# Attention and a soft mixture of experts on one core: where the next batch's rows are turned, which engine rotates the first head, and where one row maximum stands

## The chip, the cores and the metric

The kernel runs on one core of a Trainium2 chip. The metric is device time in microseconds, from the start of the program to its end. Times of single instructions come from one profiled execution.

## What is computed

Two blocks, each followed by a residual sum and a layer norm, on x of 8 batches, 1024 tokens, 128 features. The first is causal attention of 8 heads of width 128 with rotary embedding, the second a soft mixture of experts with 512 slots and a hidden width of 512. Cut to what matters:

```python
q, k, v = (einsum('bim,mhd->bhid', x, w) for w in (wq, wk, wv))
q, k = rope(q), rope(k)          # halves swapped, times sin, plus times cos
s = einsum('bhid,bhjd->bhij', q, k) / 128
p = softmax(s - 1e30 * (i < j))
x = layernorm(x + einsum('bhij,bhjd,hdm->bim', p, v, wo))
xn, se = rms_norm(x, gamma_x), rms_norm(slot_embeds, gamma_slot)
logits = einsum('bsd,etd->bset', xn, se)
slots = einsum('bsd,bset->betd', xn, softmax(logits, axis=1))
out = einsum('bnd,bsn->bsd', gelu(slots @ w1) @ w2, softmax(logits.reshape(b, s, 512)))
x = layernorm(x + out)
```

## The kernel before, in words

`attention_block` goes through 64 heads (8 batches of 8) in a pipeline, written out step by step and not as a loop on the chip. Each engine has a function `step(head)` that lists its own instructions for that step in order; the engines meet only through semaphores. So the order within each `step` is the schedule. `before` and `after` are the heads one step earlier and later. The work of a head is spread over two steps.

Products that need float32 accuracy are made of a high and a low part: ScalarE copies a PSUM result into the high part (`..._hi`), VectorE subtracts that from the same PSUM bank to get the low part (`..._lo`), and TensorE does three matmuls (`matmul_split`, L53 to L57). A PSUM bank is free for TensorE once VectorE has made the low part.

For one head, TensorE makes k and q (`project_k`, `project_q`), and their rotation is done outside: SyncE's queue swaps the halves by DMA (`swap`, L336), GpSimd multiplies k by the cosine, both swapped parts by the sine, adds, and makes both low parts (`mul_sin` L424, `rotate_add` L432, `split_lo` L440, each on 128x1024 elements). The scores of the eight row tiles of 128 queries come in fills: "s4", "s7", "s6", "s5", "s10" (tiles 1 and 0) and, in the next step, "s32". VectorE takes the row maximum (`rowmax`, L629) and ScalarE the exponential (`exp`, L511). TensorE turns the probabilities block by block (`turn`, L845) into the two banks of `ps_turn`; the fills are named "5b", "4a", "7a", "2", "5a", "3", "10", "4b", "7b", "6b", "6a" in their order, and banks alternate. Their high and low parts (L556, L656) go to `weigh_high`, `weigh_split` and `weigh_low`, which multiply by V.

V is made together with the output weights: their product is `wvo`, and `project_v` makes V for two heads. It needs x transposed, `kept.x_t`, in two copies, one for this batch and one for the next. The next batch's rows are loaded by SyncE in a batch's first step (L376). In the step of its third head (`loads_x`, `X_STEP` 2), the eight blocks are turned by `turn_x` (L853) in two halves of four blocks, into the same two banks of `ps_turn`: the first half at the end of that step, the second in the next step ahead of the scores "s32". ScalarE and VectorE split them (`split_x_hi` L561, `split_x_lo` L682), and turns "5b" and "4a" of that head come behind them, each behind a wait for `x_lo` (L919 to L922). This happens for batches 0 to 6, seven times.

Ahead of the first step stand the loading and splitting of weights, the turning of the first x, the making of `wvo`, and the first head's k, q and rotation. GpSimd does that rotation in the same order as later ones (L493 to L501).

`ffn_block` goes through 8 batches. In each, VectorE takes 8 row maxima (`find_row_peak`, L1354), the one of tile t after ScalarE's exponentials of that tile (`disped`), and between them scales the next batch's rows in two halves (`scale_rows`, L1332), behind a wait for GpSimd's norm (`norm1_known`). TensorE turns tile t once maximum t-2 is there (`turn_tile`, L1479), and turns the scaled rows of the next batch (`z_transposes`, L1465) after `z_made`, the first half after maximum 6, the second after maximum 7.

## Time and profile before

| | |
|---|---|
| median of 3 runs | 1693.78 us (1693.4 to 1696.32) |
| the profiled execution | 1695.32 us |
| its span | 1693.5 us |
| instructions | 30814 |
| TensorE busy | 1641.3 us |
| GpSimd busy | 1416.9 us |
| VectorE busy | 1217.5 us |
| ScalarE busy | 1216.6 us |
| DMA | 133.96 MB, mean 79 GB/s |

The span runs from the first to the last instruction of the profiled execution. PE is TensorE's matmuls, PEld its weight loads (they overlap), DVE VectorE, ACT ScalarE, POOL GpSimd, SP SyncE. A line of the timeline gives the start in the span, the duration, engine, line of the kernel, operation, output and inputs with shapes, the number of like instructions merged, and in brackets how long the engine was idle before and what released it. Matmuls are pipelined: one that shows 0.40 us begins 0.23 us after the one before it.

### The profile page before, as it was taken

To read this page: it belongs to the slowest core of one execution; us is meant where nothing else is said; L and a number is where in the kernel's file an instruction comes from. 1 tells how busy PE (TensorE), PEld (TensorE's weight loads), DVE (VectorE), ACT (ScalarE), POOL (GpSimd) and SP (SyncE) were. 2 spreads that over 40 slices of the span, in tenths; PEclk is the share of its full clock that TensorE was granted. 3 is DMA by queue.
4 is the path that set the end of the run, shared out by engine and by line. 5 is a ranking of instruction groups with operands and counts; after the bars stand their busy time and mean duration, and the time that the engine had idled before them with its cause. 6 is when DMAs were issued, how large, how long until landed. Compare 5 with 4: busy or idle time off the path is not lost. (4 is left out here: it accounts for less than half of the span.)

```text
span 1693.5 us, 30814 instructions
## 1 busy us (share of the span) xinstructions
PE 1641.3 (97%) x10524; PEld 1478.0 (87%) x10524; DVE 1217.5 (72%) x2891; ACT 1216.6 (72%) x2425; POOL 1416.9 (84%) x802
## 2 busy tenths in 40 slices
PE   5999999999999999999999999999999998999997
PEld 4888888888888888888888888888888886899997
DVE  3777776777777777776777777777777777677875
ACT  3777777777777777777777777777777764665664
POOL 5889988998899889998999899989988974777784
PEclk9999999999999999999999999999999999999999
DMA  4222232223222322232223222322232323223212
GB/s 146 78 70 74 76 101 62 73 78 101 62 76 75 101 73 75 75 100 76 75 75 100 75 76 76 100 76 75 75 88 76 88 76 94 51 62 94 68 31 57
DMA packets 76489, 133.96 MB, mean 79 GB/s; under 512 B 19264, under 2 KB 45888, under 8 KB 76352
## 3 DMA queue, kind: packets, MB, share of 16 engines
q1 hardware_dynamic: 74880, 130.10, 28.6%
q10 hardware_dynamic: 1472, 2.10, 0.4%
q8 instruction: 78, 1.28, 0.3%
q14 instruction: 59, 0.48, 0.1%
HBM read 56.36 MB, written 8.70 MB: 38 GB/s over the span
## 5 line engine op out<-in xcount | busy, mean ns | idle before, releaser
L511 ACT ACTIVATE probs<-ps_slot,neg_max 128x640 f32<-128x640 f32 (+7 forms) x512 | 379.3, 742 | 139.1 <-DVE neg_max L629 139.1
L629 DVE CUSTOM_DVE_ANT_0 ps_slot<-ps_slot,causal 128x640 f32<-128x640 f32 (+7 forms) x512 | 385.8, 763 | 73.3 <-PE ps_slot L57 73.3
L845 PE MATMUL ps_turn<-ident,probs 128*128 128x128 f32 x2304 | 320.4, 274 | 12.6 <-DVE x_t L682 7.6
L845 PEld LDWEIGHTS ps_turn<-ident,probs 128*128 128x128 f32 x2304 | 264.2, 140 | 43.7 <-DVE x_t L682 9.3
L55 PE MATMUL ps_slot<-k,q 128*128 128x512 f32 (+4 forms) x768 | 280.9, 366 | 2.8 <-issue 2.0
L57 PE MATMUL ps_slot<-k,q 128*128 128x512 f32 (+4 forms) x768 | 263.8, 344 | 0.0
L56 PE MATMUL ps_slot<-k,q 128*128 128x512 f32 (+4 forms) x768 | 262.8, 342 | 0.0
L656 DVE TENSOR_TENSOR pt_split<-ps_turn,pt_split 128x512 fp32r<-128x512 f32 x256 | 175.3, 685 | 93.4 <-ACT pt_split L556 93.4
L440 POOL TENSOR_TENSOR q<-rot_q,q 128x1024 fp32r<-128x1024 f32 x64 | 153.8, 2403 | 64.4 <-ACT q L539 64.4
L656 DVE TENSOR_TENSOR pt_high<-ps_turn,pt_high 128x128 fp32r<-128x128 f32 (+3 forms) x256 | 124.3, 486 | 114.5 <-ACT pt_high L556 114.5
L424 POOL TENSOR_TENSOR swapped_k<-swapped_k,rope 128x1024 f32<-128x1024 f32 x64 | 153.8, 2402 | 55.4 <-DMA swapped_k<-unrot_k 55.4
L418 POOL TENSOR_TENSOR rot_k<-unrot_k,rope 128x1024 f32<-128x1024 f32 x64 | 154.0, 2406 | 17.2 <-ACT unrot_k L521 16.6
L432 POOL TENSOR_TENSOR rot_q<-rot_q,swapped_q 128x1024 f32<-128x1024 f32 x64 | 152.7, 2386 | 9.9 <-POOL swapped_q L424 1.0
L432 POOL TENSOR_TENSOR rot_k<-rot_k,swapped_k 128x1024 f32<-128x1024 f32 x64 | 153.1, 2392 | 9.2
L55 PEld LDWEIGHTS ps_slot<-k,q 128*128 128x128 f32 x768 | 145.7, 190 | 15.5 <-issue 3.7
L556 ACT ACTIVATE pt_high<-ps_turn 128x128 fp32r<-128x128 f32 (+3 forms) x256 | 112.3, 439 | 63.9 <-PE ps_turn L845 57.8
L57 PEld LDWEIGHTS ps_slot<-k,q 128*128 128x128 f32 x768 | 144.9, 189 | 14.6
L56 PEld LDWEIGHTS ps_slot<-k,q 128*128 128x128 f32 x768 | 145.7, 190 | 11.8
L556 ACT ACTIVATE pt_split<-ps_turn 128x512 fp32r<-128x512 f32 x256 | 147.6, 602 | 10.5 <-PE ps_turn L845 10.4
L440 POOL TENSOR_TENSOR k<-rot_k,k 128x1024 fp32r<-128x1024 f32 x64 | 154.3, 2411 | 0.0
L424 POOL TENSOR_TENSOR swapped_q<-swapped_q,rope 128x1024 f32<-128x1024 f32 x64 | 153.5, 2399 | 0.0
L456 POOL TENSOR_TENSOR y_sum<-y_sum,y_head 128x1024 f32<-128x1024 f32 x55 | 131.8, 2396 | 19.3 <-issue 19.3
(174 smaller groups left out, 4300.0 us busy)
## 6 DMA issues: line engine op xcount, KB each, us to landing
swapped_k<-unrot_k SPq DMA_DIRECT2D x128, 256.0 KB, 3.6
swapped_q<-unrot_q SPq DMA_DIRECT2D x128, 256.0 KB, 3.7
inv_b<-inv_rows SPq DMA_DIRECT2D x64, 512.0 KB, 4.7
x_rows<-in_L_attn_x SPq DMA_DIRECT2D x8, 512.0 KB, 5.8
y_t<-y_sum SPq DMA_DIRECT2D x8, 512.0 KB, 5.4
x_rows<-y_t SPq DMA_DIRECT2D x8, 512.0 KB, 3.5
unrot_q<-in_L_attn_x SPq DMA_DIRECT2D x8, 512.0 KB, 5.0
row_b<-r_rows SPq DMA_DIRECT2D x16, 256.0 KB, 3.4
```

Of the source, the lines that this page charges most:

```text
L55: pe.matmul(out, stat_hi, mov_hi, start=start, stop=False, skip_group_check=True)
L56: pe.matmul(out, stat_hi, mov_lo, start=False, stop=False, skip_group_check=True)
L57: return pe.matmul(out, stat_lo, mov_hi, start=False, stop=stop, skip_group_check=True)
L418: pool.tensor_tensor(rot[1][:, :], unrot[1][:, :], kept.rope[:, 0, :], ALU.mult).then_inc(cos_made[1], 1)
L424: pool.tensor_tensor(swapped[which][:, :], swapped[which][:, :], kept.rope[:, 1, :], ALU.mult).then_inc(sin_made[which], 1)
L432: pool.tensor_tensor(rot[which][:, :], rot[which][:, :], swapped[which][:, :], ALU.add).then_inc(rotated[which], 1)
L440: pool.tensor_tensor(out[:, 1, :], rot[which][:, :], f32(out[:, 0, :]), ALU.subtract)\
L511: act.activation(probs_tile(t), score_tile(name, head, i), ACT.Exp, scale=-1.0, bias=neg_max[:, head.par, t:t + 1], accum_out=sums[:, head ...
L556: last = act.activation(hi, src, ACT.Copy)
L629: dve.tensor_tensor_reduce(tile, tile, causal[:, T - WIDTH[t]:T], -1.0, UNSEEN, ALU.add, ALU.min, neg_max[:, head.par, t:t + 1]).then_inc( ...
L656: last = dve.tensor_tensor(lo, src, f32(hi), ALU.subtract)
L845: last = pe.transpose(bank[:, at:at + P], probs_tile(t)[:, j * P:(j + 1) * P], ident[:, :])
```

## The change

In the attention half `turn_x` does both halves in one place, behind the scores "s6" of the third head's own step, in the banks that "3" and "10" of the head before have left; TensorE then waits for both low parts ahead of turn "4b". ScalarE and VectorE split the halves behind the exponentials of tile 7 and the row maximum of tile 6. The special cases in the next step, and the late "5b", are gone. In the first head, the products by the sine, the additions and the low parts of k and q go from GpSimd to VectorE, with the splits of the first V in between; ScalarE makes k's high part ahead of V's, and starts the loads of wv and wo only when the first x has landed. In the feed-forward half, row maximum 5 stands ahead of the first half of the scaling and 6 ahead of the second.

```diff
--- before.py
+++ after.py
@@ -320,7 +320,7 @@
         both_turn = ps_turn[:, :, :].rearrange("p g c -> p (g c)")
 
         def x_bank(head, half):
-            return ps_turn[:, (head.at + 1 + half) % 2, :]
+            return turn_bank(("3", "10")[half], head.step(-1))
 
         def x_half(head, half, part):
             return kept.x_t[(head.at // 8 + 1) % 2][:, part, half * BANK:(half + 1) * BANK]
@@ -493,12 +493,6 @@
             first = Head(0, 0, heads)
             pool.wait_ge(rope_landed, 32)
             mul_cos_k(first)
-            mul_sin(1, first)
-            rotate_add(1, first)
-            mul_sin(0, first)
-            rotate_add(0, first)
-            split_lo(1, first)
-            split_lo(0, first)
             steps(pool, step, 16)
 
         @block.scalar
@@ -560,8 +554,10 @@
                 act.wait_ge(x_turned, head.batch() * 2 + (half + 1))
                 act.activation(x_half(head, half, 0), x_bank(head, half), ACT.Copy).then_inc(x_hi, 1)
 
-            for n, w in (("k", wk), ("q", wq), ("v", wv)):
+            for n, w in (("k", wk), ("q", wq)):
                 act.dma_start(w_raw[n], w.rearrange("m h d -> m (h d)")).then_inc(w_landed[n], 16)
+            act.wait_ge(first_x_landed, 16)
+            act.dma_start(w_raw["v"], wv.rearrange("m h d -> m (h d)")).then_inc(w_landed["v"], 16)
             act.dma_start(w_raw["o"].rearrange("p (h m) -> p h m", h=H), wo.rearrange("h d m -> d h m"))\
                .then_inc(w_landed["o"], 16)
             act.wait_ge(first_x_turned, 1)
@@ -573,19 +569,15 @@
             act.activation(wv_t, both_turn, ACT.Copy).then_inc(wv_copied, 1)
             act.wait_ge(wvo_made, 1)
             act.activation(wvo_part(0), both_y, ACT.Copy).then_inc(wvo_hi, 1)
+            split_hi(1, first)
             split_v_hi(first.step(-2))
             split_v_hi(first.step(-1))
-            split_hi(1, first)
 
             def step(head):
                 before, after = head.step(-1), head.step(1)
                 if before.live():
                     split_v_hi(before)
-                if loads_x(before):
-                    split_x_hi(before, 1)
                 split_hi(0, head)
-                if loads_x(before):
-                    turn("5b", before)
                 turn("4a", before)
                 turn("7a", before)
                 exp("s32", before, 1)
@@ -601,6 +593,9 @@
                     act.wait_ge(z_turned, 1)
                     act.activation(kept.z_t[:, 0, :], z_slot, ACT.Copy).then_inc(z_hi, 1)
                 exp("s7", head)
+                if loads_x(head):
+                    for half in range(2):
+                        split_x_hi(head, half)
                 exp("s6", head)
                 turn("4b", head, high_done)
                 turn("7b", head)
@@ -610,10 +605,7 @@
                 exp("s10", head, 1)
                 exp("s10", head, 0)
                 turn("6a", head, split_done)
-                if loads_x(head):
-                    split_x_hi(head, 0)
-                else:
-                    turn("5b", head)
+                turn("5b", head)
 
             steps(act, step, 16)
 
@@ -716,6 +708,9 @@
                 if is_step(head, heads):
                     split_slots()
                 rowmax("s6", head)
+                if loads_x(head):
+                    for half in range(2):
+                        split_x_lo(head, half)
                 if is_step(head, heads - 1):
                     dve.wait_ge(tokens_added, 1)
                     for t in range(NT):
@@ -737,10 +732,7 @@
                         dve.tensor_tensor_reduce(kept.se_sq[:, c, :], kept.se_raw[:, c, :], kept.se_raw[:, c, :], 1.0, 0.0,
                                                  ALU.mult, ALU.add, kept.stats[:, 1, c, 0:1]).then_inc(se_squared, 1)
                 turn("6a", head)
-                if loads_x(head):
-                    split_x_lo(head, 0)
-                else:
-                    turn("5b", head)
+                turn("5b", head)
                 scale_y(1, before)
                 if is_step(head, heads):
                     dve.wait_ge(z_hi, 1)
@@ -749,14 +741,8 @@
                     dve.wait_ge(w1_hi, 1)
                     dve.tensor_tensor(kept.w1_s[:, 1, :], kept.w1_raw, f32(kept.w1_s[:, 0, :]), ALU.subtract)\
                        .then_inc(w1_lo, 1)
-                if loads_x(head):
-                    split_v_lo(head)
-                    split_x_lo(head, 1)
-                    rowmax("s32", head, 1)
-                    turn("5b", head)
-                else:
-                    split_v_lo(head)
-                    rowmax("s32", head, 1)
+                split_v_lo(head)
+                rowmax("s32", head, 1)
                 rowmax("s32", head, 0)
                 turn("4a", head)
                 scale_y(0, before)
@@ -770,6 +756,21 @@
                 dve.scalar_tensor_tensor(kept.w[:, :, lo, :], raw_w, scale, f32(kept.w[:, :, hi, :]),
                                          ALU.mult, ALU.subtract).then_inc(w_lo[n], 1)
 
+            def first_rotation(which):
+                dve.wait_ge(swap_landed[which], 32)
+                dve.tensor_tensor(swapped[which][:, :], swapped[which][:, :], kept.rope[:, 1, :],
+                                  ALU.mult).then_inc(sin_made[which], 1)
+                dve.wait_ge(sin_made[which], 1)
+                dve.wait_ge(cos_made[which], 2 - which)
+                dve.tensor_tensor(rot[which][:, :], rot[which][:, :], swapped[which][:, :],
+                                  ALU.add).then_inc(rotated[which], 1)
+
+            def first_split_lo(which):
+                dve.wait_ge(hi_made[which], 1)
+                out = qk[0][which]
+                dve.tensor_tensor(out[:, 1, :], rot[which][:, :], f32(out[:, 0, :]), ALU.subtract)\
+                    .then_inc(lo_made[which], 1)
+
             split_w("k", WK_HI, WK_LO, 1.0)
             dve.wait_ge(first_x_hi, 1)
             dve.tensor_tensor(kept.x_t[0][:, 1, :], both_y, f32(kept.x_t[0][:, 0, :]), ALU.subtract).then_inc(first_x_lo, 1)
@@ -777,10 +778,14 @@
             first = Head(0, 0, heads)
             dve.wait_ge(rope_landed, 32)
             mul_cos_q(first)
+            first_rotation(1)
             dve.wait_ge(wvo_hi, 1)
             dve.tensor_tensor(wvo_part(1), both_y, f32(wvo_part(0)), ALU.subtract).then_inc(wvo_lo, 1)
+            first_rotation(0)
             split_v_lo(first.step(-2))
             split_v_lo(first.step(-1))
+            first_split_lo(1)
+            first_split_lo(0)
             dve.wait_ge(consts, 5)
             steps(dve, step, 16)
 
@@ -848,7 +853,7 @@
 
             def turn_x(head, half):
                 pe.wait_ge(x_rows_landed, head.batch() * 16 + 16)
-                pe.wait_ge(turn_lo, head.turns(("6b", "6a")[half]))
+                pe.wait_ge(turn_lo, head.step(-1).turns(("3", "10")[half]))
                 for t in range(4 * half, 4 * half + 4):
                     last = pe.transpose(x_bank(head, half)[:, t % 4 * P:(t % 4 + 1) * P], kept.x_rows[:, t, :],
                                         ident[:, :])
@@ -896,8 +901,7 @@
 
             def step(head):
                 before, after = head.step(-1), head.step(1)
-                if not loads_x(before):
-                    turn("5b", before, ("6b", before))
+                turn("5b", before, ("6b", before))
                 free_slot(exped[5], before)
                 if head.live() and not before.live():
                     pe.wait_ge(cos_made[0], head.made() * 2)
@@ -912,16 +916,8 @@
                 free_slot(exped[1], before)
                 if before.live():
                     pe.wait_ge(lo_made[0], before.made())
-                if loads_x(before):
-                    turn_x(before, 1)
                 scores("s32", before)
-                if loads_x(before):
-                    pe.wait_ge(x_lo, before.batch() * 2 + 1)
-                    turn("5b", before)
-                    pe.wait_ge(x_lo, before.batch() * 2 + 2)
-                    turn("4a", before)
-                else:
-                    turn("4a", before, ("6a", before))
+                turn("4a", before, ("6a", before))
                 turn("7a", before, ("5b", before))
                 weigh_high(before, (0, 1))
                 free_slot(v_lo, before, -2, -2, 2)
@@ -953,7 +949,12 @@
                 turn("10", before, ("5a", before))
                 free_slot(exped[4], head)
                 scores("s6", head)
+                if loads_x(head):
+                    for half in range(2):
+                        turn_x(head, half)
                 weigh_split(before)
+                if loads_x(head):
+                    pe.wait_ge(x_lo, head.batch() * 2 + 2)
                 if is_step(head, heads):
                     pe.wait_ge(z_made, 1)
                     for t in range(NT):
@@ -968,8 +969,6 @@
                 turn("6b", head, ("4b", head))
                 weigh_low(before)
                 turn("6a", head, ("7b", head))
-                if loads_x(head):
-                    turn_x(head, 0)
 
             pe.wait_ge(consts, 5)
             pe.wait_ge(first_x_landed, 16)
@@ -1407,13 +1406,13 @@
                 find_row_peak(b, par, 2, first)
                 find_row_peak(b, par, 3, first)
                 find_row_peak(b, par, 4, first)
+                find_row_peak(b, par, 5, first)
                 if ahead:
                     dve.wait_ge(norm1_known, b + 1)
                     scale_rows(1 - par, half_tiles(0))
-                find_row_peak(b, par, 5, first)
+                find_row_peak(b, par, 6, first)
                 if ahead:
                     scale_rows(1 - par, half_tiles(1)).then_inc(z_made, 1)
-                find_row_peak(b, par, 6, first)
                 find_row_peak(b, par, 7, first)
                 scale_slots(b)
                 if ahead:
```

## Rows read from the trace of the kernel before

**Rows 1.** the page: busy time, share of the span and instructions of each engine

```profile
PE 1641.3 (97%) x10524; PEld 1478.0 (87%) x10524; DVE 1217.5 (72%) x2891; ACT 1216.6 (72%) x2425; POOL 1416.9 (84%) x802
```

**Rows 2.** waits of TensorE, 45 to 1400 us: waiter <- awaited: us, times, longest

```profile
PE ps_turn L845 <- DVE x_t L682: 7.6, 7, 1.1
```

**Rows 3.** stretches: us, then busy us of PE, PEld, DVE, ACT, POOL; clock, DMA

```profile
225.92:247.09 21.17, 21.17 (x134) 19.03 (x133) 15.51 (x35) 16.25 (x35) 19.04 (x9) 1.00 0.36 100
247.09:270.92 23.83, 22.49 (x142) 19.88 (x141) 16.72 (x37) 17.35 (x37) 19.15 (x9) 1.00 0.26 67
```

**Rows 4.** timeline, TensorE, third step of batch 1: start, us, what, idle before

```profile
264.22 0.38 PE L845 MATMUL ps_turn<-ident,probs 128*128 128x128 f32 x2
265.70 0.66 PE L845 MATMUL ps_turn<-ident,probs 128*128 128x128 f32 x4 [1.09 <-DVE x_t L682]
266.60 0.63 PE L845 MATMUL ps_turn<-ident,probs 128*128 128x128 f32 x4 [0.24 <-DVE pt_high L656]
266.98 0.48 PE L55 MATMUL ps_y<-pt_high,v 128*128 128x512 f32 x1
```

**Rows 5.** timeline, TensorE, the same step, around tile 6's scores

```profile
252.95 0.40 PE L55 MATMUL ps_y<-pt_split,v 128*128 128x512 f32 x1
255.73 0.71 PE L845 MATMUL ps_turn<-ident,probs 128*128 128x128 f32 x5
```

**Rows 6.** timeline, VectorE, the same stretch of that step

```profile
252.31 1.21 DVE L656 TENSOR_TENSOR pt_low<-ps_turn,pt_low 128x512 fp32r<-128x512 f32 x3
253.44 1.09 DVE L629 CUSTOM_DVE_ANT_0 ps_slot<-ps_slot,causal 128x896 f32<-128x896 f32 x1
256.40 0.29 DVE L656 TENSOR_TENSOR pt_high<-ps_turn,pt_high 128x128 fp32r<-128x128 f32 x1 [1.82 <-ACT pt_high L556]
```

**Rows 7.** timeline, ScalarE, the same stretch of that step

```profile
252.51 1.13 ACT L511 ACTIVATE probs<-ps_slot,neg_max 128x1024 f32<-128x1024 f32 x1
254.62 1.01 ACT L511 ACTIVATE probs<-ps_slot,neg_max 128x896 f32<-128x896 f32 x1 [0.89 <-DVE neg_max L629]
```

**Rows 8.** timeline, first head: GpSimd, VectorE and TensorE, in order of time

```profile
20.75 2.34 POOL L424 TENSOR_TENSOR swapped_k<-swapped_k,rope 128x1024 f32<-128x1024 f32 x1 [1.93 <-DMA swapped_k<-unrot_k]
21.95 1.22 DVE L781 TENSOR_TENSOR wvo_all<-ps_y,wvo_all 128x1024 fp32r<-128x1024 f32 x1 [3.88 <-ACT wvo_all L575]
28.73 0.65 PE L55 MATMUL ps_slot<-x_t,w_all 128*128 128x512 f32 x1 [2.37 <-DVE v L664]
35.20 1.29 DVE L648 TENSOR_TENSOR rot_q<-ps_slot,rope 128x512 f32<-128x512 f32 x2 [6.52 <-POOL q L440]
36.63 0.77 PE L55 MATMUL ps_slot<-k,q 128*128 128x512 f32 x1
```

**Rows 9.** stretches of the first head, columns as in Rows 3

```profile
28.50:35.00 6.50, 4.61 (x12) 3.31 (x12) 0.18 (x1) 2.68 (x3) 6.50 (x3) 0.74 0.20 40
35.00:39.20 4.20, 3.99 (x12) 3.21 (x13) 2.18 (x4) 1.48 (x3) 4.20 (x3) 0.59 0.56 142
```

**Rows 10.** groups of VectorE instructions by shape: busy us, mean ns | idle before

```profile
L682 DVE TENSOR_TENSOR x_t<-ps_turn,x_t 128x512 fp32r<-128x512 f32 x14 | 9.5, 680 | 0.0
L750 DVE TENSOR_TENSOR wvo_all<-unrot_k,wvo_all 128x512 fp32r<-128x512 f32 x1 | 0.7, 692 | 0.0
L1439 DVE TENSOR_SCALAR out_row<-res,neg_mean,rstd 128x128 f32<-128x128 f32 x8 | 3.9, 553 | 0.0
```

**Rows 11.** groups of ScalarE instructions by shape, columns as in Rows 10

```profile
L561 ACT ACTIVATE x_t<-ps_turn 128x512 fp32r<-128x512 f32 x14 | 8.4, 598 | 0.0
```

**Rows 12.** timeline, feed-forward half: VectorE and TensorE, batches 2 and 3

```profile
1497.96 0.70 DVE L1354 CUSTOM_DVE_ANT_0 ps_turn<-ps_turn,peak_b 128x512 f32<-128x512 f32 x1 [0.61 <-ACT disp L1260]
1501.95 0.70 DVE L1354 CUSTOM_DVE_ANT_0 ps_turn<-ps_turn,peak_b 128x512 f32<-128x512 f32 x1
1502.81 1.04 PE L1465 MATMUL ps_turn<-ident,z_row_other 128*128 128x128 f32 x8
...
1533.58 0.66 PE L1481 MATMUL ps_turn<-ident,logits 128*128 128x128 f32 x4 [0.74 <-DVE row_peak L1354]
```

## The prediction

> **What bounds the kernel now.** I read the page first [rows 1]: TensorE is busy for 97% of the span, every other engine for 84% or less, so a microsecond counts only if TensorE stands still in it or if TensorE's own list grows or shrinks. Next came TensorE's waits through the attention half [rows 2]: one line stands out, the turns of probabilities (L845) waiting for the split of the next batch's rows (L682), 7 times, at most 1.1 us each. Seven is the number of steps that turn rows (the third head of batches 0 to 6). Then I put two stretches side by side [rows 3]: an ordinary step takes 21.17 us and TensorE is busy for all of it; the row-turning step beside it takes 23.83 us with 22.49 busy. The row-turning step costs 2.66 us more, which seven times is 18.6 us, and this is where most of the change acts. The rest is in the first 50 us and in the feed-forward half.
>
> **Part 1, rows turned behind tile 6's scores.** Where do the 2.66 us go? After the scores of tiles 3 and 2, TensorE does two turns, stands 1.09 us for `x_lo`, does four, stands 0.24 us, does four [rows 4]. Four turns in an unbroken list take 0.38 us to the next instruction, two 0.19, so from 264.22 to 266.98 (2.76 us) only 10 turns or 0.95 us are work: 1.81 us are stall and restart. The remaining 0.85 us are the eight row turns themselves, in two groups. The eight stay in the kernel: twice 0.38 us, and the matmul behind a group takes 0.48 us [rows 4] where one in a run takes 0.40 [rows 5], so 0.84; I take the measured 0.85.
> What is added is two waits for a bank and one for the splits. The banks: after tile 6's scores end at 252.95 [rows 5] the first four turns need the lower split of "3", the second four that of "10". VectorE does these as three instructions from 252.31 to 253.52 [rows 6]; the first, 512 wide like the 0.68 us of [rows 10], ends about 253.0, and with the release TensorE is held about 0.1 us. So four turns run from 253.06 to 253.44, TensorE stands until 253.58, four more run to 253.96, and a restart costs a little: 0.3 us of stall. The step then costs 0.85 + 0.3 = 1.15 us over an ordinary one, in place of 2.66: 1.51 us saved, seven times 10.6 us. Bounds: with no stall at all 1.81 each or 12.7 us; with twice the stall and 0.3 us more behind it 0.9 each or 6.3 us.
> What hides the splits? ScalarE ends the exponentials of tile 7 at 253.6 [rows 7], takes the first half at 253.7, the second at 254.2 (0.60 us each [rows 11]) and is free at about 254.7 for the exponentials of tile 6, which started at 254.62 [rows 7]: under 0.1 us late. VectorE ends tile 6's row maximum at 254.5 [rows 6] and does two splits of 0.68 us [rows 10], to 255.7, in a stretch where it sat idle for 1.82 us before 256.40 [rows 6]. TensorE meanwhile weighs the lower tiles, 2.78 us from 252.95 to 255.73 [rows 5], now shifted to end at 256.9. The wait for `x_lo` before "4b" has therefore 1.1 us to spare. Queued behind that wait are turns "4b" and "7b" and the scores of tile 5. If the cover went, each microsecond over 1.1 would cost 7 us. Nothing of the load moves on SyncE: the rows are asked for two steps earlier and are now read within the same step, some 7 us sooner. ScalarE and VectorE lose their special order at the step's end; turns "5b", "4a" and "7a" take their ordinary places, where [rows 3] shows TensorE fully busy.
>
> **Part 2, the first head's rotation on VectorE.** Before, the first scores wait for GpSimd's chain: its first product of swapped k starts at 20.75, after the DMA, and six GpSimd instructions of 2.34 us and more later VectorE is released by the split of q, 6.52 us idle, at 35.20 [rows 8]. After, VectorE does these. Its price for a 1024-wide all-SBUF pair is about 1.2 us: 0.692 us for 512 columns [rows 10], and 1.22 us for 1024 with one side in PSUM [rows 8]. k's product and addition run from 20.7 to 23.1. Behind them is queued the lower split of the combined V and O weights, which started at 21.95 [rows 8], now about 23.15, 1.2 us later; TensorE's V products and, behind their splits, head 1's projections (28.73 [rows 8]) go later by the same 1.2 us, to 29.9. TensorE was busy for 4.61 us from 28.50 to 35.00 at a clock of 0.74 [rows 9], nearly all of it these projections; at that clock they end at about 34.4; k's and q's lower splits, two more of 1.2 us behind V's own lower splits (which release the projections at 29.9), are done by about 32.3 and no longer bind. q's raw copy and its cosine product follow (1.6 us), so tile 7's scores start at about 36.0 where they started at 36.63 [rows 8]: 0.6 us earned. Then the clock: the granted clock was 0.59 from 35.00 to 39.20 [rows 9], behind a stretch in which TensorE stood waiting for this chain. About 0.8 of the 4.2 us ran at the upper level, so the low level cost some 1.7 us. That is the lower of its two levels, 1.2 instead of 2.4 GHz. With the pause gone I expect the upper one there in some executions; against that the pause before the V products grows by 1.2 us and may lower the clock for those. Worth: between 3.5 us gained (both well) and 1.5 us lost (the low level in the V products and again in the scores). I take 1.2 us gained, nearer the case in which one low stretch is exchanged for another.
> ScalarE's move of two weight loads behind the arrival of x lets x compete with less, but its two issues and the table load then stand ahead of x's first split. No row shows either alone; I take nothing for it, 0.5 us either way in the bounds, since each side is some tenths of a microsecond.
> The Trainium skill, "SBUF: State Buffer", section "SBUF: two separate sides", speaks against this part: a VectorE instruction with two SBUF inputs and a GpSimd instruction that reads SBUF take turns at one port pair, the loser waiting for the whole of the other. By that rule each such meeting costs up to one GpSimd instruction; that is rival E.
>
> **Part 3, row maximum 5 ahead of the scaling.** It shortens one wait: TensorE stood 0.74 us before turning tile 7 in batch 3, where GpSimd's norm was late [rows 12]; for the smaller delays of the other batches I allow 0.3 us more. It adds one: maximum 5 needs the exponentials of tile 5, and VectorE, which already waited 0.61 us for tile 4's [rows 12], now waits as long again, 0.6 to 0.7 us, instead of scaling meanwhile. In batch 2 maximum 7 then ends not at 1501.95 + 0.70 = 1502.65 but at about 1503.3, and the second half of the z turns, due some 0.4 us after 1502.81 [rows 12], stands 0.1 to 0.2 us; so in five batches. Gain 1.0, loss 0.9: I take 0.1 us gained; bounds 1.3 gained (no stall) and 1.2 lost.
>
> **The sum.** 10.6 + 1.2 + 0.1 = 11.9 us. The profiled execution took 1695.32 us, its span of 1693.5 and 1.8 us around it, so it would come to 1683.4; it is 1.5 us above the median of the runs shown, 1693.78, and 11.9 us off that median are my forecast: **1681.9 us**.
>
> **The rivals.**
> A, the stall only moves: the new waits together with late exponentials of tile 6 cost 0.6 us per step more than I count. For it: two bank waits are as tight as 0.1 us and everything hangs on VectorE's place. Against: ScalarE and VectorE both show room. Part 1 then gives 7 x 0.91 = 6.4 us: 1693.78 - 6.4 - 1.3 = 1686.1.
> B, the clock is kind: no low level in the first 50 us, 3.5 instead of 1.2 us, and part 1 at its best: 1693.78 - 12.7 - 3.5 = 1677.6. For it: the low levels there follow pauses that shrink. Against: one pause grows.
> C, the change does not do what it says: turns behind tile 6's scores stand for their banks as long as the old ones stood for `x_lo`, 1.8 us each. Then part 1 gives nothing: 1693.78 - 1.3 = 1692.5.
> D, slower: the wait for `x_lo` before "4b" becomes the bound. It decides once the splits land more than 1.1 us later than I place them; from there each microsecond costs 7. To be slower than before by over 0.2% (3.4 us) it would need 1.1 + 1.51 + (3.4 + 1.3)/7 = 3.3 us of lateness, as with both splits behind the exponentials of tile 6 and the turns "4b". At 3.5 us: 1693.78 + 7 x 0.9 - 1.3 = 1698.8. Nothing in the two engines' lists points to that.
> E, VectorE is held in the first head: one of its six moved instructions waits for a GpSimd instruction of 2.34 us [rows 8] because both read two SBUF inputs. All behind it goes that much later, and part 2 loses 1.2 us instead of gaining them: 1693.78 - 10.6 + 1.2 - 0.1 = 1684.3. For it: a 128-wide scaling from SBUF took 553 ns [rows 10], nearly the 692 ns of a pair four times as wide, while GpSimd subtracted. Against: GpSimd has only k's cosine product ahead of 20.75 [rows 8] and then itself waits for k's lower split and for head 1's raw k.
>
> **How the numbers follow.** Forecast 0.58, A 0.17, B 0.11, C 0.06, D 0.03, E 0.05. A difference of 0.2%, 3.4 us, is about what a measurement of this kernel can tell from no change, so the line is at 1690.4. Forecast, A, B and E are faster, 0.91; C is the same, 0.06; D slower, 0.03. The range has to hold 8 in 10: the forecast's own bounds reach from about 1679 to 1686, A adds its neighbourhood up to 1687.5, and on B's side the range ends at 1677.8, which leaves out its better half, C and D: 1677.8 to 1687.5.
>
> **What the changed profile would show.** The row-turning steps should last 22.3 us (22.0 to 22.9), TensorE waiting in them twice for the lower splits of "3" and "10", each under 0.2 us, and never for L682's successor; "4b" should follow the weighing at once. If it waits there, A or D holds. The first wait of over 1 us that I expect is ahead of the V products, with VectorE's rotation before it; tile 7's first scores should start between 34.5 and 37.5 us. In the feed-forward half the wait ahead of tile 7's turn should be gone, and small ones stand at the z turns. The forecast would be wrong if ordinary steps no longer took 21.17 us, since 57 of them multiply any error.

## The result

Both kernels were timed on one chip in five executions each: before 1693.78 us in the median (1693.38 to 1696.32), after **1684.88 us** (1684.58 to 1687.97). The ratio is 0.9947, with a 95% interval of 0.9933 to 0.9962: 9.0 us less, between 6.4 and 11.3. The forecast was 1681.9 us in a range of 1677.8 to 1687.5. The range holds the result; the forecast itself is 3.0 us too low. Two of the 23 executions of the kernel before in the first session of experiments were disturbed (2340 and 4392 us) and are left out of its times and ratios.

The profiled execution took 1684.79 us, its span 1683.0. To see where the time went I cut both spans at ScalarE's raw k copies, one for each head (the timeline of ScalarE, L521 before and L515 after):

| stretch | before | after | difference | the prediction |
|---|---|---|---|---|
| start to head 2's raw k copy | 52.90 | 53.46 | +0.56 | -1.2 (part 2) |
| from there to head 63's copy | 1309.99 | 1299.68 | -10.31 | -10.6 (part 1) |
| from there to the end | 330.61 | 329.86 | -0.75 | -0.1 (part 3) |

The page of after (busy us, share, instructions, beside [rows 1]):

```profile
PE 1641.3 (98%) x10524; PEld 1478.1 (88%) x10524; DVE 1223.4 (73%) x2897; ACT 1216.7 (72%) x2425; POOL 1402.0 (83%) x796
```

TensorE's busy time is what it was to 0.1 us, in a span 10.5 us shorter. What fell is its standing still. Its waits from 45 to 1400 us (us, times, longest) no longer name the splits of the rows, which [rows 2] put at 7.6 us. They show two for exponentials, where the kernel before has one of 0.8 us in the same stretch:

```profile
PE ps_turn L850 <- ACT probs L505: 1.9, 2, 1.1
PE ps_slot L55 <- DVE swapped_q L694: 0.8, 1, 0.8
PE ps_turn L850 <- DVE pt_high L648: 0.8, 1, 0.8
```

The two stretches that answer to [rows 3], an ordinary step and the row-turning step behind it (columns as there):

```profile
223.95:245.13 21.18, 21.18 (x133) 19.04 (x133) 15.52 (x35) 16.25 (x34) 19.05 (x8) 1.00 0.37 100
245.13:267.44 22.31, 22.29 (x141) 19.73 (x141) 16.60 (x37) 17.27 (x36) 17.77 (x8) 1.00 0.27 72
```

The ordinary step is unchanged; the other fell from 23.83 to 22.31 us. And TensorE, VectorE and ScalarE in that step, beside [rows 4 to 7]:

```profile
251.86 0.34 PE L57 MATMUL ps_slot<-k,q 128*128 128x384 f32 x1
252.22 1.16 PE L858 MATMUL ps_turn<-ident,x_rows 128*128 128x128 f32 x8
...
253.13 0.49 PE L55 MATMUL ps_y<-pt_split,v 128*128 128x512 f32 x1
...
256.00 0.71 PE L850 MATMUL ps_turn<-ident,probs 128*128 128x128 f32 x5
...
251.39 1.21 DVE L648 TENSOR_TENSOR pt_low<-ps_turn,pt_low 128x512 fp32r<-128x512 f32 x3
...
253.53 1.28 DVE L674 TENSOR_TENSOR x_t<-ps_turn,x_t 128x512 fp32r<-128x512 f32 x2
...
256.68 0.29 DVE L648 TENSOR_TENSOR pt_high<-ps_turn,pt_high 128x128 fp32r<-128x128 f32 x1 [1.87 <-ACT pt_high L550]
...
252.89 1.13 ACT L555 ACTIVATE x_t<-ps_turn 128x512 fp32r<-128x512 f32 x2
253.91 1.00 ACT L505 ACTIVATE probs<-ps_slot,neg_max 128x896 f32<-128x896 f32 x1
```

The eight turns stand directly behind tile 6's scores and are over by 253.13: 0.91 us where an unbroken list of eight would take 0.75, after some 0.17 us of standing ahead of them (252.05, when the next scores would start, to 252.22). Both splits are over by 254.8, and turns "4b" follow the weighing at 256.00 without a wait.

### The profile page after: what moved, and what is told of

It is laid out like the page before. It is cut to its first block and busy times, and to the rows that moved or that the text cites. A ratio compares the mean times of both kernels' runs of the same rounds, so it can differ in the third digit from the quotient of the medians.

```text
span 1683.0 us, 30814 instructions
## 1 busy us (share of the span) xinstructions
PE 1641.3 (98%) x10524; PEld 1478.1 (88%) x10524; DVE 1223.4 (73%) x2897; ACT 1216.7 (72%) x2425; POOL 1402.0 (83%) x796
## 5 line engine op out<-in xcount | busy, mean ns | idle before, releaser
L55 PE MATMUL ps_slot<-k,q 128*128 128x512 f32 (+4 forms) x768 | 279.8, 364 | 1.7 <-DVE swapped_q L694 0.8
L55 PEld LDWEIGHTS ps_slot<-k,q 128*128 128x128 f32 x768 | 145.3, 189 | 14.1 <-issue 1.4
```

The source lines that it names most:

```text
L55: pe.matmul(out, stat_hi, mov_hi, start=start, stop=False, skip_group_check=True)
```

## The experiments

Kernels were timed in three sessions, the third on another chip; each has its own executions of the kernel before, and ratios are taken within a session. The measure throughout is the ratio with its interval for the whole, and the trace for the place.

**Each part alone.** Four kernels apply parts of the change to the kernel before: part 1; part 2; part 3; and parts 1 and 3. Their edits are the hunks of the diff shown above.

> Part 1 alone (rows turned behind tile 6's scores; first head and row maximum as before). My theory: each of the seven row-turning steps goes from 23.8 to 22.3-22.4 us and nothing else moves, so 7 x 1.47 = 10.3 us less than before, 1683.5 us. Rival, the shorter step only brings a later wait forward (in the feed-forward half, which begins earlier): less than 9 us are left at the end, 1685 us or more, with the missing time in the feed-forward half.

> Part 2 alone (first head's rotation on VectorE, the two weight loads moved). Theory, VectorE's list: the first head up to head 2's raw k copy takes 0.5 us or so longer than before (53.4-53.5 instead of 52.9), because V products and head 1's projections go later and GpSimd's rotation of head 1's k is late for head 1's tile 5; result within 0.7 us of before, slightly slower. The prediction's reading: 1.2 us faster. Rival, interplay: the loss in the kernel after comes only from part 2 together with part 1, then head 2's raw k copy stands below 52.5 here.

> Part 3 alone (row maximum 5 ahead of the scaling). Theory from the two traces: 0.75 us less in the stretch from head 63's raw k copy to the end of the span, most of it the 0.74 us wait ahead of tile 7's turn in batch 3, and nothing before it. The prediction said 0.1 us. Rival: those 0.75 us come from the shift of the whole half by part 1; then this kernel's stretch is as long as before's within 0.2 us.

> Parts 1 and 3 with the first head as before. Theory, part 2 is worth -0.5 us (a loss): this kernel takes 0.3 to 1 us less than the kernel after, with head 2's raw k copy at 52.9 us. The prediction's reading, part 2 gains 1.2 us: it takes 1.2 us more than the kernel after.

| kernel | median us (executions) | ratio to before, 95% |
|---|---|---|
| before | 1692.92 (21) | 1 |
| part 1 alone | 1683.21 (4) | 0.9931 (0.9915 to 0.9948) |
| part 2 alone | 1694.09 (12) | 1.0010 (1.0000 to 1.0019) |
| part 3 alone | 1694.15 (10) | 1.0003 (0.9994 to 1.0012) |
| parts 1 and 3 | 1683.09 (6) | 0.9939 (0.9927 to 0.9952) |

Part 1 is the whole gain: its row-turning steps take 22.3 us, and neither half behind it gives anything back. Part 2 costs 1.7 us by the ratio, somewhere between nothing and 3.2. Part 3 cannot be told from nothing. My expectation for it fell: I had read the 0.75 us of the table above as its gain, with the last stretch at 329.86. Alone it gave 328.8 us there, 1.8 less than before, but the seven z turns (the turns of the scaled rows, between which part 3 acts) did not come closer together. From the first to the seventh of them pass 196.36 us before, 196.57 with part 1 alone and 196.25 with part 2 alone; with part 3 it is 195.68 (after), 196.44 (alone) and 196.58 (parts 1 and 3). The means are 196.39 and 196.23; the eight profiles of the later sessions, all with part 3, have 197.14 to 198.89, so this distance moves by more than part 3 could.

**Much of what moves the rest is the clock.** I went through each profile in stretches of 1 us and added, wherever the granted clock is under 1.00, busy TensorE time times the share of the clock that is missing. Before has four low stretches, worth 1.68, 1.67, 1.71 and 1.71 us; after four, 6.3 us in all; part 1 alone four, part 3 alone three, part 2 alone and parts 1 and 3 two each, 3.3 us. That is what takes part 3's last stretch down by 1.8 us: it has one low stretch there where before has two, and without them 327.1 and 327.2 us are left.

The clock is not all of it. The kernel after, run again in the second session, took 333.78 us from head 63's copy to the end, 3.9 more than the same code in the table above; its low stretches there are worth 4.5 us against 3.0, and 2.4 us are left over. TensorE's waits from 1400 us on show 1.7 of them, first after, then after again:

```profile
PE ps_turn L1480 <- DVE row_peak L1353: 0.4, 1, 0.4
PE ps_turn L1464 <- DVE z_row_other L1331: 0.4, 1, 0.4
...
PE ps_turn L1480 <- DVE row_peak L1353: 1.6, 3, 0.6
PE ps_turn L1464 <- DVE z_row_other L1331: 1.0, 1, 1.0
```

The waits for row maxima stand ahead of tile 2 in batches 1, 2 and 7, which needs maximum 0, ahead of everything that part 3 moves. Why VectorE comes late there in one execution and not in the other stays open.

In the attention half the clock matters by its place. The first head of part 3 alone, the same instructions as before's, has its low stretches elsewhere (us, TensorE busy, clock; first part 3 alone, then parts 1 and 3, with the same first head again):

```profile
24.00:28.00 4.00, 3.58 (x17) 0.57 0.00 0
31.00:35.00 4.00, 3.57 (x9) 0.57 0.00 0
```

```profile
24.00:28.00 4.00, 2.46 (x21) 1.00 0.00 0
29.00:33.00 4.00, 4.00 (x11) 0.57 0.00 0
```

With one code, head 2's raw k copy then comes at 53.68 or at 51.69; the kernel before, with low stretches at 28 to 33 and 35 to 40 [rows 9], is at 52.90. For parts 1 and 3 I had expected 52.9. So the +0.56 us of my table cannot be read as the price of part 2. Two profiles have to be compared that have the low clock in the same place. Part 2 alone and parts 1 and 3 are such a pair (one low stretch each, from 29 to 33 or 34).

**The first head, clock aside.** The first kernel here is parts 1 and 3 (rotation on GpSimd), the second part 2 alone (on VectorE); ScalarE, TensorE, GpSimd, in order of time:

```profile
31.49 1.02 ACT L521 ACTIVATE unrot_k<-ps_slot 128x1024 f32<-128x1024 f32 x1
36.57 0.47 PE L55 MATMUL ps_slot<-k,q 128*128 128x512 f32 x1 [0.31 <-ACT unrot_q L532]
39.88 2.36 POOL L432 TENSOR_TENSOR rot_k<-rot_k,swapped_k 128x1024 f32<-128x1024 f32 x1
42.54 1.07 ACT L539 ACTIVATE k<-rot_k 128x1024 fp32r<-128x1024 f32 x1
45.11 0.41 PE L835 MATMUL ps_turn<-ident,probs 128*128 128x128 f32 x2 [0.18 <-DVE pt_high L652]
```

```profile
29.84 0.79 PE L55 MATMUL ps_slot<-x_t,w_all 128*128 128x512 f32 x1 [2.37 <-DVE v L660]
32.81 1.03 ACT L515 ACTIVATE unrot_k<-ps_slot 128x1024 f32<-128x1024 f32 x1 [3.33 <-PE ps_slot L57]
35.96 0.47 PE L55 MATMUL ps_slot<-k,q 128*128 128x512 f32 x1 [0.69 <-DVE rot_q L644]
38.13 2.36 POOL L424 TENSOR_TENSOR swapped_k<-swapped_k,rope 128x1024 f32<-128x1024 f32 x1 [1.77 <-DMA swapped_k<-unrot_k]
40.64 2.39 POOL L432 TENSOR_TENSOR rot_k<-rot_k,swapped_k 128x1024 f32<-128x1024 f32 x1
43.06 1.06 ACT L533 ACTIVATE k<-rot_k 128x1024 fp32r<-128x1024 f32 x1 [1.00 <-POOL rot_k L432]
45.43 0.44 PE L860 MATMUL ps_turn<-ident,probs 128*128 128x128 f32 x2 [1.15 <-ACT probs L505]
```

Tile 7's scores, the second fill of the first head (L55 from k and q), start 0.61 us earlier, as forecast. But head 1's projections come 1.0 us later and its raw k copy 1.3 us, and behind that copy runs a chain which the change left on GpSimd: cosine product, the swap's DMA, sine product, addition; then ScalarE's upper split of head 1's k, which stands in ScalarE's queue **ahead of the exponentials of tile 5**. ScalarE waits 1.00 us for GpSimd, the exponentials wait with it, and TensorE stands 1.15 us where it stood 0.18. Head 2's raw k copy follows at 52.05 instead of 51.69: 0.6 earned, 1.0 lost.

Other profiles give this loss its bounds. Counted from head 0's raw k copy, which takes out when x landed, head 2's copy comes after 36.45 us with the old rotation (parts 1 and 3) and after 36.66 to 36.79 with the new one (part 2 alone, and halves apart and turns late below), each with one low stretch. With two, within 24 to 29 and 31 to 36 us, it comes after 38.21 and 38.25 with the old rotation (part 1 alone, part 3 alone) and after 38.26 and 38.23 with the new (after, twice). There is no loss there, since with that clock the old rotation waits too, as the table below shows. In the first head part 2 loses 0.2 to 0.4 us or nothing, by where the low clock lies.

For part 2 alone I had expected the copy at 53.4 to 53.5 and had named a copy below 52.5 as the mark of a loss that needs part 1 as well. The measured 52.05 meets that mark, but the mark left the clock out: halves apart has part 1 too and one low stretch, and its copy comes at 52.05 as well.

If the chain is the cause of the wait, the wait must depend on one thing only, the lead: the time from head 1's raw k copy to the start of tile 7's scores. Over all profiles with ScalarE's queue as it was in that place:

| kernel | raw k, head 1 | scores | lead | TensorE's wait |
|---|---|---|---|---|
| halves apart (below) | 32.78 | 35.83 | 3.05 | 1.29 |
| turns late (below) | 32.52 | 35.60 | 3.08 | 1.15 |
| part 2 alone | 32.81 | 35.96 | 3.15 | 1.15 |
| part 3 alone (GpSimd rotates) | 34.39 | 37.56 | 3.17 | 1.14 |
| after | 34.17 | 37.40 | 3.23 | 1.10 |
| after, again | 33.90 | 37.21 | 3.31 | 1.07 |
| part 1 alone (GpSimd rotates) | 34.30 | 37.82 | 3.52 | 0.83 |
| first head reordered (below) | 31.25 | 34.85 | 3.60 | 0.79 |
| reordered, halves apart | 31.38 | 35.26 | 3.88 | 0.39 |
| V's load back (below) | 33.86 | 37.94 | 4.08 | 0.18 |
| extra work on GpSimd (below) | 36.56 | 40.65 | 4.09 | 0.21 |
| parts 1 and 3 | 31.49 | 36.57 | 5.08 | 0.18 |
| before | 31.55 | 36.63 | 5.08 | 0.18 |

The wait is 4.2 to 4.4 us less the lead, until only 0.18 is left. Part 1 alone and part 3 alone, each with the old rotation, are on the same line: there the low clock on the V products had eaten the lead. So GpSimd's rotation is not safe from this chain either; the new one in the order of the kernel after has 3.05 to 3.38 us of lead, unless something else delays the scores.

**Mending it, three ways.** All start from the kernel after. The first reorders VectorE's list so that V products and head 1's projections keep their old times:

```
-            first_rotation(1)
+            first_sin(1)
             dve.wait_ge(wvo_hi, 1)
             (lower split of the combined weights)
-            first_rotation(0)
+            first_add(1)
+            first_sin(0)
             split_v_lo(first.step(-2))
             split_v_lo(first.step(-1))
+            first_add(0)
```

and ScalarE splits V ahead of k. The second puts four of the eight row turns behind the first products that weigh the split tiles, away from the bank that is not free:

```
-                    for half in range(2):
-                        turn_x(head, half)
-                weigh_split(before)
+                    turn_x(head, 0)
+                    weigh_split(before, (0,))
+                    turn_x(head, 1)
+                    weigh_split(before, (1, 2, 3))
```

The third is both.

> The kernel after, unchanged, as the measure for the three beside it. Theory, the first head is worth a small loss: 1684.5 to 1685.5 us, and its TensorE has 2 to 4 stretches of the low clock, each worth 1.6 to 1.7 us.

> The kernel after with VectorE's list of the first head reordered (the lower split of the combined weights behind k's product, V's lower splits ahead of q's addition; ScalarE splits V ahead of k as before), so that V products and head 1's projections keep the times they had before. Theory, the loss lies in these standing 1.0 us later and GpSimd's chain for head 1's k behind them: the wait of 1.1 us for tile 5's exponentials goes, and the kernel takes 1.5 to 2 us less than the kernel after. Rival, the loss is the low clock and not the chain: the same within 0.5 us in the median, and the first head differs only by the place of the low stretches.

> The kernel after, with the second group of four row turns put behind the first four of the 16 products that weigh the split tiles. Theory, the second bank wait then finds the bank free: a row-turning step takes 22.0 to 22.1 us in place of 22.3, 1.5 to 2 us less in all. Rival, the wait for the lower split takes it back since x's second half is split later: steps stay at 22.3 us.

> Both edits of the two kernels ahead. If they add up, 3 to 4 us less than the kernel after; if one is covered by the other or by the clock, no more than the better of the two.

| kernel | median us (executions) | ratio to before, 95% | row-turning step |
|---|---|---|---|
| before | 1697.04 (11) | 1 | |
| after | 1687.04 (5) | 0.9941 (0.9929 to 0.9954) | 22.3 |
| first head reordered | 1685.70 (6) | 0.9943 (0.9930 to 0.9956) | 22.3 |
| halves apart | 1686.89 (5) | 0.9943 (0.9930 to 0.9956) | 22.25 |
| both | 1684.98 (5) | 0.9930 (0.9917 to 0.9943) | 22.26 |

The kernel after came out at 1687.04 us and not at 1684.5 to 1685.5; the kernel before came out 4.1 us slower beside it than in the first experiments, and only the ratio can be compared. The reordered head does in part what I expected. V products and head 1's projections are back at 23.18 and 28.68 us, and with one low stretch each, head 2's raw k copy comes at 50.56 and 50.59 us, against 52.05 with the order of the kernel after. But the wait for tile 5's exponentials does not go: 0.79 us of it are left, since tile 7's scores come earlier as well and the lead is still 3.60. In the time of the whole, 1.5 to 2 us of gain were expected and the ratio shows none, as the rival said; with halves apart it shows 1.9. Five or six executions that differ by 3 to 5 us among themselves cannot settle this, and I take only the trace's reading as shown.

Halves apart fell short: 22.25 us and not 22.0 to 22.1, 0.5 us over seven steps in the trace and nothing in the time. The second group of turns stands behind three of the twelve products; "four of the 16" was a miscount. TensorE:

```profile
80.30 0.63 PE L858 MATMUL ps_turn<-ident,x_rows 128*128 128x128 f32 x4
80.68 0.48 PE L55 MATMUL ps_y<-pt_split,v 128*128 128x512 f32 x1
81.00 0.39 PE L56 MATMUL ps_y<-pt_split,v 128*128 128x512 f32 x1
81.22 0.39 PE L57 MATMUL ps_y<-pt_split,v 128*128 128x512 f32 x1
81.46 0.60 PE L858 MATMUL ps_turn<-ident,x_rows 128*128 128x128 f32 x4
81.81 0.48 PE L55 MATMUL ps_y<-pt_split,v 128*128 128x512 f32 x1
82.13 0.39 PE L56 MATMUL ps_y<-pt_split,v 128*128 128x512 f32 x1
```

The second bank wait is gone (81.22 to 81.46 is the ordinary distance). But behind each group of turns the first product holds the next back by 0.32 us instead of 0.23: a second group buys a second restart of 0.09 us with the 0.16 us of wait that it saves. Neither of my two expectations had that. No wait for the later split appears either.

**The prediction's rivals D and E, and two edits more.** The turns behind all the weighing, so that nothing covers the splits:

```
                 scores("s6", head)
+                weigh_split(before)
                 if loads_x(head):
                     for half in range(2):
                         turn_x(head, half)
-                weigh_split(before)
```

Extra work on GpSimd beside VectorE's first rotation (`y_sum` is read by nobody yet):

```
+            pool.memset(y_sum[:, :], 0.0).then_inc(consts, 1)
+            pool.wait_ge(consts, 6)
+            for i in range(3):
+                pool.tensor_tensor(y_sum[:, :], y_sum[:, :], y_sum[:, :], ALU.add).then_inc(consts, 1)
+                pool.wait_ge(consts, 7 + i)
```

The load of V's weights back in its old place:

```
-            for n, w in (("k", wk), ("q", wq)):
+            for n, w in (("k", wk), ("q", wq), ("v", wv)):
                 act.dma_start(...)
             act.wait_ge(first_x_landed, 16)
-            act.dma_start(w_raw["v"], wv.rearrange("m h d -> m (h d)")).then_inc(w_landed["v"], 16)
```

And, on the kernel with both mends, the chain cut where it meets ScalarE, in the first head alone:

```
-                split_hi(1, after)
+                if not is_step(head, 0):
+                    split_hi(1, after)
                 turn("6b", head)
                 exp("s5", head)
+                if is_step(head, 0):
+                    split_hi(1, after)
```

> The kernel after, with the eight row turns put behind the 12 products that weigh the split tiles, directly ahead of the wait for x_lo and of turns 4b. Theory, the cover of the splits is the weighing: without it TensorE waits ahead of 4b for two splits of 0.6 us on ScalarE and the last of VectorE's, some 2 us after the turns, so row-turning steps take 24.0 to 24.6 us, longer than the 23.8 of before (rival D of the prediction made real). Rival, the splits are never in the way since both engines have room: 22.1 to 22.5 us.

> The kernel after, with four more instructions on GpSimd in the first head, a fill and three 1024-wide additions of about 2.4 us each in a row between its first product and head 1 (extra work on a buffer that nobody reads yet), so that GpSimd reads SBUF all through VectorE's first rotation. Rival E: VectorE's products and additions of 1.23 us each are held for up to 2.4 us apiece, or GpSimd's additions become longer, and V products start several us later. My theory, no such turn-taking shows: 1.2 to 1.3 us each, within 0.1 us of one another, V products at 24.2-24.4 us as in the kernel after.

> The kernel after, with the load of the V weights issued directly behind K's and Q's again, not behind the arrival of x. Theory, the move is worth nothing: x's first split, k's raw copy and the V products stand within 0.2 us of the kernel after, the time within 0.5 us. Rival, the load competes with x: x's turns start 0.3 us later or more.

> The two edits of the kernel with both, and in the first head alone ScalarE's upper split of head 1's k put behind the exponentials of tile 5. If the wait ahead of those exponentials comes from ScalarE queued behind GpSimd's rotation of head 1's k, TensorE's wait for them (0.4 us there, 1.1 us in the kernel after) goes to 0.2 or less and head 2's raw k copy comes 0.2 to 0.4 us earlier than 50.6 for the same place of the low clock. Rival, the exponentials were late by themselves: no change.

*Turns late:* 1694.97 us in one execution, beside 1696.00 in the median of before. Its row-turning steps take 23.8 us, as long as before's, 0.2 short of what I expected. The cover is real:

```profile
82.54 1.03 PE L858 MATMUL ps_turn<-ident,x_rows 128*128 128x128 f32 x8
85.15 0.77 PE L850 MATMUL ps_turn<-ident,probs 128*128 128x128 f32 x5 [1.57 <-DVE x_t L674]
```

Without 2.8 us of weighing between the turns and "4b", 1.57 us of wait come back in each of the seven steps, and with them all of part 1.

*Extra work on GpSimd:* my theory fell. The one execution took 1690.41 us. GpSimd, its three additions asked for one at a time, and VectorE:

```profile
19.64 1.89 POOL L499 TENSOR_TENSOR y_sum<-y_sum 128x1024 f32<-128x1024 f32 x1
21.61 2.75 POOL L499 TENSOR_TENSOR y_sum<-y_sum 128x1024 f32<-128x1024 f32 x1
24.45 2.75 POOL L499 TENSOR_TENSOR y_sum<-y_sum 128x1024 f32<-128x1024 f32 x1
...
20.54 2.08 DVE L766 TENSOR_TENSOR swapped_k<-swapped_k,rope 128x1024 f32<-128x1024 f32 x1 [2.63 <-DMA swapped_k<-unrot_k]
22.65 2.80 DVE L770 TENSOR_TENSOR rot_k<-rot_k,swapped_k 128x1024 f32<-128x1024 f32 x1
25.37 1.21 DVE L788 TENSOR_TENSOR wvo_all<-ps_y,wvo_all 128x1024 fp32r<-128x1024 f32 x1
26.51 1.77 DVE L766 TENSOR_TENSOR swapped_q<-swapped_q,rope 128x1024 f32<-128x1024 f32 x1
28.32 1.22 DVE L770 TENSOR_TENSOR rot_q<-rot_q,swapped_q 128x1024 f32<-128x1024 f32 x1
```

The three instructions that read two operands from SBUF while GpSimd adds take 2.08, 2.80 and 1.77 us; the one that reads an operand from PSUM takes 1.21 in the middle of it, and the one after GpSimd's end 1.22. V products start at 26.64 instead of 24.24.

The ends show what holds them. GpSimd's additions end at 21.53, 24.36 and 27.20 us, and the three VectorE instructions end at 22.62, 25.45 and 28.28: each about 1.1 us after the addition beside which it began, nearly its whole 1.23. It waits for the rest of that addition and then does its own work, so it lost 0.5 to 1.6 us, by how much of the addition was left. GpSimd waits in turn: its first addition takes 1.89 us, and the two that begin while VectorE is at work take 0.86 more, though GpSimd's durations are rough in these profiles. This agrees with the rule of the Trainium skill, "SBUF: State Buffer", section "SBUF: two separate sides", that whichever of the two instructions starts first has the port pair until its end.

*V's load back:* x's first turn on TensorE starts at 7.93 us and k's raw copy at 15.21, against 15.20 in the kernel after. All profiles together say more than this one. With the load in its old place, behind K's and Q's, the first turn starts at 7.93 to 8.15 us (before, part 1, part 3, parts 1 and 3, and this kernel); in the nine profiles with the load moved it starts at 7.63 to 7.93, in each session 0.1 to 0.3 us earlier than the others, and head 0's raw k copy comes at 14.99 to 15.29 instead of 15.21 to 15.43. So the move seems to earn 0.1 to 0.2 us, less than the rival's 0.3 and more than my nothing; it rests on five profiles against nine and not on this experiment alone. The time was 1684.13 us (4 executions), ratio 0.9927 (0.9912 to 0.9942), beside the 0.9941 of the kernel after in the session before it; the intervals overlap, and 0.2 us is far below what they can tell.

*k's upper split late:* the wait for tile 5's exponentials fell to the floor although the lead was 3.38 us, for which the table would give 0.9:

```profile
45.09 0.63 PE L857 MATMUL ps_turn<-ident,probs 128*128 128x128 f32 x4 [0.76 <-DVE pt_high L651]
45.90 0.41 PE L857 MATMUL ps_turn<-ident,probs 128*128 128x128 f32 x2 [0.18 <-DVE pt_high L651]
```

From head 1's raw k copy to head 2's it takes 18.56 us, against 19.2 to 19.3 in every other kernel with the new rotation. That is 0.7 us earned by the order of one instruction, more than the 0.2 to 0.4 that I expected, because the low clock had cut this profile's lead. The copy itself stands at 52.56, with two low stretches; the place that I had named, ahead of 50.6, was for a profile with one, so it was not tested. Time 1684.44 us (5 executions), ratio 0.9929 (0.9915 to 0.9943). This and the kernel with both mends are the best that I measured in which all is kept; each by about 2 us below the kernel after by the ratio, within what the intervals leave open.

## Why the prediction was right

**Part 1 was right.** Expected: a step of 22.3 us, about 0.3 us of stall, 1.51 us saved, seven times 10.6. Measured: 22.31 to 22.37 us, 0.33 us of stall (0.17 ahead of the turns, 0.16 within them), 10.31 saved; alone, 0.9931. The reading that carried it was the comparison of two neighbouring stretches [rows 3] and the count of what in 2.76 us is work [rows 4]. The splits landed at 254.8, 1.2 us ahead of "4b"; I had said 1.1 to spare. One term was small by a little: tile 6's exponentials came 0.2 us late (253.91, where before's 254.62 would fall on 253.72 by the end of the scores) and not under 0.1, and nothing waited for them. Turns late shows that this margin is what the part rests on, and that D would have been a return to before's step of 23.8 us.

**Part 2 failed in one step.** What I costed happened: the combined weights' split at 22.96 in the kernel after (said 23.15), and in part 2 alone, where the low clock lies much as before, V products and head 1's projections about a microsecond later (29.84 for 29.9) and tile 7's scores at 35.96 (said 36.0). The step that failed is "tile 7's scores start at about 36.0: 0.6 us earned". It ends the sum at the first scores and takes their start for the head's end. I had moved head 1's projections back by 1.2 us and asked who waits for them only as far as TensorE's own next scores; GpSimd's chain for head 1's k and ScalarE's queue behind it had lost 1.9 us of lead, from 5.08 to 3.15, where about 4.1 are needed, and 1.0 us came back as a wait. The clock term, the other 0.6 us of the 1.2, was not there either: with either rotation profiles show low stretches in the first 50 us, one or two, with the new one also a double one. I took nothing for the loads' move, with 0.5 us either way; it seems to earn 0.1 to 0.2. So part 2 loses 0.4 us in one matched pair of traces (52.05 for 51.69) and nothing in the other placement of the clock, and 0 to 3.2 us in the timed runs, in place of 1.2 gained.

**Part 3 was small, as forecast, with one term too low.** Both of its halves are in the traces. The gain: from tile 6's turn to tile 7's it takes 1.33 us in every batch of all eleven profiles with part 3; without it these distances are longer by 1.10 us in all in the kernel before, where 0.74 of it is the wait of [rows 12], and by 1.38 and 1.12 with part 1 alone and part 2 alone. I had said 1.0. The loss: the z turns, 1.04 us long in [rows 12], take 1.22, since the second four stand for maximum 7:

```profile
1491.94 0.69 DVE L1353 CUSTOM_DVE_ANT_0 ps_turn<-ps_turn,peak_b 128x512 f32<-128x512 f32 x1
...
1492.19 1.22 PE L1464 MATMUL ps_turn<-ident,z_row_other 128*128 128x128 f32 x8
```

I had put down 0.9 us, in five batches. It is in all seven that turn a next batch's rows: in the kernel after 0.11 us in the first and 0.17 to 0.28 in the others, 1.3 us together. So the two halves come to about 0.2 us lost and not 0.1 gained, which no time here can tell from nothing.

**The rivals.** A (the stall only moves) and C (no effect) are excluded by the steps of 22.3 us. B, no low clock in the first 50 us, was seen in no profile. C's condition, row turns that stand for their banks as long as the old ones stood for `x_lo`, is not met either: they stood 0.33 us. D and E are real mechanisms with the price that their experiments gave, and both are kept off here: D by the weighing, E because GpSimd does nothing from 18.7 to 35.3 us in the kernel after. The result lies near E's 1684.3, but for another reason: VectorE's instructions there take 1.21 to 1.23 us throughout, none of them held. The 553 ns that spoke for E [rows 10] are a mean of unlike instructions: the first two of the eight scalings take 0.86 and 1.58 us, while GpSimd subtracts until 1680.41 (L1207), and the six after its end 0.33 each. The mean hid two instructions in the trace of before that look held. A loss in the first head with the right size is no proof of the mechanism that I had named for it.

**The 3 us between forecast and result** are then 1.2 to 1.6 us from part 2 (nothing or 0.4 lost for 1.2 gained), 0.3 from part 1 and 0.3 from part 3; the remaining microsecond is less than the interval, 6.4 to 11.3 us, leaves open. Executions of one kernel here differ by 3 to 7 us. Profiles differ by the number and length of their low-clock stretches, most of them 1.5 to 1.7 us each, and by waits in the feed-forward half that the clock does not explain. That the range holds the result is part 1's doing; the other two parts both came out below their forecasts.

## What to carry to other kernels

When work moves to an engine with room, follow what is now later to its last user in every queue, not only to the next instruction of the bounding engine: the loss was in a chain that the diff does not touch, behind one instruction that stood ahead of more urgent work. Lead times make such a chain plain: one table of lead against wait over several kernels showed a threshold that no single profile did. Before a microsecond between two profiles is explained, look where the low clock lies in each, and use every profile that matches, not one pair. And read a group's mean as a mean: one held instruction can hide in it.

## What the runs showed of the hardware

The place of the low clock is not a property of the code. The same first head had it at 24 to 28 and 31 to 35 us, at 28 to 33 and 35 to 40, or at 29 to 33 alone; in each it is the lower of the two levels, 1.2 instead of 2.4 GHz, for 3 to 4 us. A difference shows as early as the first projections, whose last 512-wide group begins with a product of 0.63 us in the kernel after and of 0.39 us in part 2 alone at nearly the same time, though the granted clock reads 1.00 in both:

```profile
16.24 0.63 PE L55 MATMUL ps_slot<-x_t,w_all 128*128 128x512 f32 x1
```

```profile
16.19 0.39 PE L55 MATMUL ps_slot<-x_t,w_all 128*128 128x512 f32 x1
```

In 13 of the 14 profiles the next low stretch falls on the V products where this product is slow (0.58 or 0.63 us), and on head 1's projections where it is not (0.39 to 0.46). Extra work on GpSimd is the exception: 0.40 us, and a low stretch from 25 to 33 us. What sets it remains open.

An instruction on VectorE with two operands in SBUF takes up to 2.3 times as long beside GpSimd's additions (2.80 us for 1.22), because the two take turns, and GpSimd's addition grows from 1.89 to 2.75 us by the same turns; an instruction with an operand in PSUM does not take part (1.21 us). I had not expected this from the traces of before.
